# Two attentions with narrow heads: turning whole rows and stacking their parts through DRAM, against stacking in SBUF and turning the stacks

## The reference

```python
# layer 1 (the normed layer): LayerNorm over each head of 32 columns on q and k,
# the last 16 context rows form a second softmax whose result is added
q = _ln((x @ Wq + bq).reshape(b, s1, H, HD), qn_w, qn_b)          # H = 16, HD = 32
k = _ln(kv[..., :HD], kn_w, kn_b)
ctx = _attn(qT, k.transpose(0, 2, 1, 3), v.transpose(0, 2, 1, 3)) # softmax(q k' * HD**-0.5) v
...
# layer 2 (the rotary layer): q and k are rotated by tables of positions
q = apply_axial_rope((x @ Wq).reshape(b, n, 32, 16), pos_map)
k = apply_axial_rope(k.reshape(b, ctx_n, 32, 16), ctx_pos_map)
logits = jnp.einsum('bqhd,bkhd->bhqk', q, k) * scale
```

## Time and profile before

| what | us |
|---|---|
| three runs | 3720.03, 3726.92, 3727.14 (median 3726.92) |
| profiled execution: its span | 3721.0 |
| normed layer, one block in the steady part (1403.6 to 1549.6 is 6 blocks) | 24.33 |
| rotary layer, one block in the steady part (2243.1 to 2469.1 is 8 blocks) | 28.25 |
| normed layer, from its first load to its first scores | 53.0 (1245.7 to 1298.7) |
| rotary layer, from its first projection to its first scores | 26.3 (2110.9 to 2137.2) |

### The profile page before, as it was taken

One profiled execution on the slowest core, in us unless ns is written; L12 is line 12 of the kernel. 1 busy time (PEld: TensorE's weight loads), 2 busy tenths in 40 slices (PEclk: granted clock), 3 DMA queues, 4 the chain that ended last, 5 costly groups with the idle time before them and its releaser, 6 DMA issues.

```text
span 3721.0 us, 62085 instructions
## 1 busy us (share of the span) xinstructions
PE 3407.3 (92%) x23446; PEld 2808.9 (75%) x23446; DVE 2348.9 (63%) x4621; ACT 1666.9 (45%) x3641; POOL 1308.3 (35%) x1239
## 2 busy tenths in 40 slices
PE   7999999959999689988999899997889999999977
PEld 6899999937777456656998645554689999999865
DVE  6677777763323478866444466665667777777766
ACT  5666665531211155542222255554245555555531
POOL 1013334111243477732222356665422222222212
PEclk9999999978999899998999999999889999999989
DMA  3246665124645100001111000000000000000001
GB/s 130 80 135 222 225 227 181 42 80 168 241 176 188 69 27 28 11 5 69 35 35 38 1 4 3 4 3 19 28 6 18 13 18 18 18 7 19 12 1 48
DMA packets 94869, 246.53 MB, mean 66 GB/s; under 512 B 14448, under 2 KB 18672, under 8 KB 89840
## 3 DMA queue, kind: packets, MB, share of 16 engines
q1 hardware_dynamic: 88336, 222.12, 17.3%
q0 software_dynamic: 6240, 20.45, 1.6%
HBM read 364.95 MB, written 70.52 MB: 117 GB/s over the span
## 4 chain that ended last, share of the span: by engine, by line
PE 39%; DVE 6%; issue 3%; ACT 2%; POOL 2%; DMA 0%; SPq 0%; POOLq 0%; DVEq 0%; ACTq 0%
PE banks L104 34%; PE banks L214 4%; ACT P L78 1%; DVE xn L92 0%; POOL kst L87 0%; DVE X L87 0%; DVE st L270 0%; DVE PL L87 0%; DVE X L95 0%; POOL rs L87 0%; DVE KL L95 0%; DVE P L91 0%; ACT nkT L81 0%; POOL CL L87 0%; DVE XL L87 0%
## 5 line engine op out<-in xcount | busy, mean ns | idle before, releaser
L87 DVE TENSOR_TENSOR X<-X,banks 128x512 f32<-128x512 f32 x352 | 239.7, 682 | 192.9 <-PE banks L104 192.7
L98 DVE TENSOR_REDUCE nmx<-banks 128x4 f32<-128x1024 f32 (+2 forms) x256 | 239.1, 955 | 153.6 <-PE banks L104 151.6
L104 PE MATMUL banks<-XH,wqh 128*128 128x256 f32 x1024 | 291.9, 285 | 0.0
L104 PE MATMUL banks<-XL,wqh 128*128 128x256 f32 x1024 | 286.2, 279 | 0.0
L104 PE MATMUL banks<-XH,wql 128*128 128x256 f32 x1024 | 286.1, 279 | 0.0
L87 POOL TENSOR_TENSOR slo<-sraw,shi 128x512 fp32r<-128x512 f32 x96 | 126.9, 1322 | 379.3 <-ACT shi L81 351.2
L104 PE MATMUL banks<-XH,tT 128*128 128x256 f32 x1024 | 248.1, 286 | 8.8 <-DVE XL L87 5.9
L78 ACT ACTIVATE nPT<-banks 128x1024 f32<-128x1024 f32 x192 | 196.0, 1021 | 114.4 <-PE banks L104 113.9
L104 PE MATMUL banks<-XL,tT 128*128 128x256 f32 x1024 | 246.7, 284 | 0.0
L104 PE MATMUL banks<-woh,OH 128*128 128x512 f32 x512 | 219.2, 428 | 13.1 <-DVE OL L87 11.1
L78 ACT ACTIVATE P<-banks,nb,qst 128x256 f32<-128x256 f32 x256 | 141.0, 560 | 190.8 <-DVE nb L87 190.7
(11 more groups left out here) (435 smaller groups left out, 10480.5 us busy)
## 6 DMA issues: line engine op xcount, KB each, us to landing
WU<-expert_parts SPq DMA_DIRECT2D x39, 4096.0 KB
WD<-expert_parts SPq DMA_DIRECT2D x39, 2048.0 KB
sraw<-in_moe_w SPq DMA_DIRECT2D x96, 256.0 KB, 3.2
expert_parts<-shi SPq DMA_DIRECT2D x96, 256.0 KB
expert_parts<-slo SPq DMA_DIRECT2D x96, 256.0 KB
wqr<-in_L_xattn_Wq SPq DMA_DIRECT2D x16, 512.0 KB, 4.3
wor<-in_L_xattn_Wo SPq DMA_DIRECT2D x16, 512.0 KB, 5.5
sraw<-in_L_ffn_factors SPq DMA_DIRECT2D x32, 256.0 KB, 3.1
```

The costliest lines, as they stand in the source:

```text
L87: return self.e.tensor_tensor(out, a, b, op)
L98: return self.e.tensor_reduce(out, a, AX.X, op, **kw)
L104: return self.e.matmul(out, l, r, start=start, stop=stop, skip_group_check=skip)
```

## The change

Rows are turned plain, and split after. For each tile and kind (`kt`, `qt`) TensorE turns the 512 columns in one group of four, 32 groups or 128 turns a layer; ScalarE copies the group out of bank 7 twice, raw and rounded; POOL subtracts (`kl`, `ql`) to get the low part; SP writes high and low to a DRAM tensor `turned_parts` (`kw`, `qw`: two DMAs of 256 KB each, 512-byte rows). For each block SP then loads the stripes from DRAM into `nkT` and `nqT` (`rd`): 6 DMAs onto 32 partitions each (normed), 12 DMAs onto 16 partitions each (rotary), 1.57 MB a block either way, in rows of 1 KB. `rd` waits until both tiles' parts have landed and until the `st` steps of the block before the last are done; the first scores of the block wait for all of its loads. The selector stripes are made by POOL once and loaded into `nkT` at the start of the layer. The places of many steps change with it.

```diff
-            "k0": (-28, -20.5), "k1": (-28, -20), "q0": (-24.5, -18), "q1": (-22, -17), "q2": (-18.5, -13.5),
-            "k2": (-16, -14), "q3": (-18, -8), "k3": (-15, -5), "kp": -50, "krd": -49.5, "krp": -39.5, "qp": (-41, -39),
+            "kt": -47.5, "kl": -46.5, "kw": -45, "qt": -44.5, "ql": -43.5, "qw": -42, "rd": -17.5,
+            "kp": -56.5, "krd": -56, "krp": -53.5, "qp": (-53.5, -51.5), "qrd": -51.5, "qrp": -49, "vp": -17, "vb": -16,
...
+        self.TD = nc.dram_tensor("turned_parts", (2, NB, 2, 512, S), F32, kind="Internal").ap()
...
-    def wait_block(self, e, L, p, blk):
-        for q in "kq":
-            last = max(self.W[L]["turn"][f"{q}{2 + blk // 4}", (p // 2 * 2 + i, p % 2)] for i in range(2))
-            e.wait_ge(self.S["n_e" + q], last + 1)
+    def wait_block(self, e, L, p):
+        e.wait_ge(self.S[f"rd{p % 2}"], (96 if L == 1 else 192) * (p // 2 + 1))
+
+    def sp_parts(self, sp, L, kind, t):
+        S, b, i = self.S, t // 2, t % 2
+        dst = self.TD[0 if kind == "k" else 1][b].rearrange("a (c p) n -> p a c n", p=128)[:, :, :, 128 * i:128 * i + 128]
+        sp.wait_ge(S["n_lo" + kind], t + 1)
+        for a in range(2):
+            sp.dma(dst[:, a], self.parts_of(L, kind)[0][:, a].bitcast(F32)).then_inc(S[f"{kind}w{i}"], 16)
+
+    def sp_stacks(self, sp, L, p):
+        S, w, l1 = self.S, self.W[L], L == 1
+        b, hh = p // 2, p % 2
+        n = 32 if l1 else 16
+        for kind in "kq":
+            for i in range(2):
+                sp.wait_ge(S[f"{kind}w{i}"], 32 * (b + 1))
+        sp.wait_ge(S["n_st"], w["U"] * (p - 1))
+        for kind, tile, parts in (("k", "kT", (0, 1, 0)), ("q", "qT", (0, 0, 1))):
+            dst = w[tile][:, p % 2, :, :].bitcast(F32)
+            for s, a in enumerate(parts):
+                src = self.TD[0 if kind == "k" else 1][b, a, 256 * hh:256 * hh + 256, :].rearrange("(m e d) n -> e d m n", m=8, d=n)
+                for e in range(1 if l1 else 2):
+                    sp.dma(dst[64 * e + n * s:64 * e + n * s + n], src[e]).then_inc(S[f"rd{p % 2}"], 16)
...
-            if step in ("k1", "q1"):
...
-                pool.tt(part[2], src, part[0].bitcast(F32), ALU.subtract).then_inc(S["n_loq" if kind == "q" else "n_lok"], 1)
+            if step in ("kl", "ql"):
+                parts, raw = self.parts_of(L, step[0])
+                pool.wait_ge(S["n_e" + step[0]], t + 1)
+                pool.tt(parts[:, 1], raw[:], parts[:, 0].bitcast(F32), ALU.subtract).then_inc(S["n_lo" + step[0]], 1)
...
-            if step in ("k2", "k3", "q2", "q3"):
...
-                    x = (w["stq"] if q else w["stk"][:, t[0] % 2, :])[:, 512 * i + 128 * a:512 * i + 128 * a + 128].bitcast(F32)
-                    x = self.turn(pe, banks[7][:, 128 * a:128 * a + 128], x)
+            if step in ("kt", "qt"):
+                rows = self.rows_of(L, step[0], t)
+                self.wait_rows(pe, L, step[0], t)
+                self.wait_turned(pe, L, w["before7"][step, t])
+                for a in range(4):
+                    x = self.turn(pe, banks[7][:, 128 * a:128 * a + 128], rows[:, a, :])
...
+            if step in ("kt", "qt"):
+                kind = step[0]
+                parts, raw = self.parts_of(L, kind)
+                act.wait_ge(S["n_t" + kind], t + 1)
+                act.wait_ge(S["n_lo" + kind], t)
+                act.acopy(raw[:], z7)
+                if t:
+                    act.wait_ge(S[f"{kind}w{(t - 1) % 2}"], 32 * ((t + 1) // 2))
...
+                act.acopy(parts[:, 0], z7).then_inc(S["n_e" + kind], 1)
```

More of the change, by code:

```diff
@@ L161, in __init__ @@
         self.S = Sems(nc)
-        for name, first in (CHOICE_ON | CTX_ON).items():
+        for name, first in (CHOICE_ON | CTX_ON | TURNED_ON).items():
             self.S[name] = self.S[first]
@@ L1605, in narrow_list @@
                 put(base + at["mt"][i], "mt", (p, i))
-                for kind in ("k0", "k1", "k2", "k3", "q0", "q1", "q2", "q3"):
-                    put(base + at[kind][i] + first(kind, 2 * p + i), kind, (p // 2 * 2 + i, p % 2))
+            put(base + at["rd"], "rd", p)
         for t in range(NT):
@@ L1631, in narrow_before @@
         w["steps"] = self.narrow_list(L)
-        w["before6"], w["before7"], w["rope"], w["stack"], w["turn"] = {}, {}, {}, {}, {}
+        w["before6"], w["before7"], w["rope"] = {}, {}, {}
         last6 = last7 = None
@@ L1935, in wait_turned @@
             e.wait_ge(S["xh"], ln_at(2, a))
-        elif kind[0] == "q":
-            e.wait_ge(S["n_eq"], self.W[L]["turn"][use] + 1)
         else:
-            e.wait_ge(S["n_ek"], self.W[L]["turn"][use] + 1)
+            e.wait_ge(S["n_eq" if kind == "qt" else "n_ek"], a + 1)
     def wait_rows(self, e, L, kind, t):
@@ L1997, in sp_narrow @@
         back = self.OS[1:2 * T + 1, :].rearrange("(k t p) d -> t p k d", k=2, p=128)
+        m = 3 if l1 else 2
+        sp.wait_ge(S["n_sel"], m)
+        sel = w["sel"][:].rearrange("p j n -> p (j n)").unsqueeze(1)
+        keys = w["kT"][:].bitcast(F32).rearrange("p a (c j) n -> p (a c) (j n)", j=4)
+        for first, n in ((96, 8),) if l1 else ((48, 4), (112, 4)):
+            sp.dma(keys[first:first + n], sel.to_broadcast([n, 4, 1024])).then_inc(S["sel"], 16)
         for step, a in w["steps"]:
@@ L2013, in sp_narrow @@
                     sp.dma(dst[112:116], src[4:8].unsqueeze(1).to_broadcast([4, 4, 256])).then_inc(S[f"xs{k}"], 16)
+            if step in ("kw", "qw"):
+                self.sp_parts(sp, L, step[0], a)
+            if step == "rd":
+                self.sp_stacks(sp, L, a)
             if step == "mix":
@@ L2058, in pool_narrow @@
         k = 16 if l1 else 32
[L2059 to L2079 removed]
+        sel = w["sel"]
+        pool.e.memset(sel[:], 0.0).then_inc(S["n_sel"], 1)
+        pool.wait_ge(S["n_sel"], 1)
+        for first, c in ((0, slice(0, 240)), (4, slice(240, 256))) if l1 else ((0, slice(0, 256)),):
+            pool.e.affine_select(out=sel[:, :, c], in_=sel[:, :, c], compare_op=ALU.not_equal, fill=1.0, base=-first,
+                                 pattern=[[-1, 4], [0, c.stop - c.start]], channel_multiplier=1).then_inc(S["n_sel"], 1)
         if not l1:
@@ L2161, in pe_narrow, with heads @@
                              else wkv[:, c, 512 * e:512 * e + 512])
-        heads = lambda u: ((slice(0, 128), 2 * u), (slice(0, 128), 2 * u + 1)) if l1 else ((slice(0, 64), u), (slice(64, 128), u))
+        def heads(u, n):
+            return ((slice(0, n), 2 * u), (slice(0, n), 2 * u + 1)) if l1 else ((slice(0, n), u), (slice(64, 64 + n), u))
         for step, t in w["steps"]:
@@ L2290, in act_narrow @@
                 if t >= 8:
-                    act.wait_ge(S["n_loq"], max(w["stack"]["q", (t - 8, hh)] for hh in range(2)) + 1)
+                    act.wait_ge(S["n_tq"], t - 7)
                 act.wait_ge(S["ln_turned"], ln_at(2, t))
```

127 lines of the change are left out of this document (31 added, 96 removed), and 5 rows, old and new, of the table PLACES.

## The result

The changed kernel takes 3829.8 us (median of 4 runs, 3822.8 to 3832.7) against 3723.5 (3717.3 to 3727.1) for the kernel before: ratio 1.0284, 95% interval 1.0271 to 1.0297. It is 106 us slower. The forecast was 3708, 19 under the median of 3726.9 that it started from. The profiled execution has a span of 3830.8 us, 109.8 more than before's 3721.0.

A forecast was written before the change was run, and what follows sets the result against it. TensorE, busy nearly throughout both layers' steady blocks, was taken as the bound; -63 (rotary turns) + 43 (load wait) + 17 (rotary start) - 16 (normed layer) = -19 us, so 3702 profiled and 3708 measured, range 3660 to 3768.

The forecast's parts named there:

- Turns removed, rotary: Rotary layer, TensorE: 96 fewer turn groups and 16 waits for ScalarE's bank 7 copy gone, -63 us, 3.9 a block.
- Wait for the stack loads: Rotary blocks, before first scores: loads arrive after 13.6 us against 10.5 of cover, 3.1 us wait in 14 blocks, +43 us.
- Cover in the normed layer ... No wait, as long as SP is not late: Normed blocks: about 14 us of TensorE work covers stack loads taking 9.5 us in all, so no wait.
- 4 us lie between `mt` and its use: Maxima's DMAs queue behind the stack loads, but 4 us in the list before their use were to hide this.
- Normed body: Normed layer's blocks: 22.0 us each instead of 24.33, VectorE and POOL close behind TensorE; -33 us.
- keeps nothing: Rival: VectorE, POOL and SP's queue hold the normed block at 24.3 us; +14 in all, 3741 us, chance 0.17.
- Normed start: Normed layer up to first scores: first turn 12 us later, `qt0` ahead of `qp1` 7 more; sum +17, bounds 8 to 25.
- Rotary start: Rotary layer up to first scores: turn, copies, low part, write and 12 loads come first; +17 us, between 8 and 25.
- Serial loads: Rival: rotary loads run one after another, 6.7 us wait before each block's first scores; +36, 3763 us, chance 0.28.
- No wait at all: Rival: stack loads land as fast as issued, so rotary blocks never wait; -66, 3661 us, chance 0.15.

The follow-up runs named there:

- e6: e4 with each stack load cut into two halves, the first sent earlier, TensorE waiting only for the half it needs; ratio 0.9941 to the kernel before.
- e7: e4 with the same stack-load bytes sent onto three times as many partitions, so stacks hold other rows; ratio 0.9966 to the kernel before.
- e10: e8 with the normed layer's first turned scores of a half block moved behind the next half block's scores; 3692.0 us, ratio 0.9917 to the kernel before.
- e3: Changed kernel with SP issuing the loads of expert output earlier, later ones ahead of the stack loads; ratio 1.0140 to the kernel before.
- e2: Changed kernel with the maxima's DMAs issued by ScalarE behind its own copy instead of by SP; ratio 1.0253 to the kernel before.
- e8: Edits of e5 and e6 together, first normed loads at a place of their own; 3694.2 us, ratio 0.9902 to the kernel before.
- e5: e4 with first tiles' turn, low-part and store steps and first rotary stack loads moved in both layers' starts; ratio 1.0050 to the kernel before.
- e4: Changed kernel with the edits of e2 and e3 together; ratio 1.0109 to the kernel before.

## Why the prediction was wrong, step by step

- **Turns removed, rotary (-63).** Direction right, size wrong: without late loads the body is 39 us shorter (e6, e7, e10 agree within 0.5), 2.55 a block and not 3.9. TensorE's busy time fell by 2.55 us a block (219.66 / 8 to 199.23 / 8), not by the 3.20 that six groups take from start to start: start to start, the other instructions take 0.65 us a block more than beside the turns. And the 0.69 us wait for the copy out of bank 7 brought nothing: idle time is 0.79 us a block before and 0.80 after, now most of it for VectorE's nOT. I had subtracted a wait and not asked who is late next.
- **Wait for the stack loads (+43).** The mechanism, the place and the arrival were right: 13.6 us after the first issue, data of about 12.0 us (2420.2 to 2432.2), the last with some luck. The wait is 2.4 us a block (16.9 / 7) instead of 3.1, as the cover at this place was 12.1 us (2418.86 to 2430.92), not 10.5; 1.1 of it was a wait for VectorE's nOT, the attention's output. Over the body the loads cost 56 us (451.4 against 395.8), of which 40 are TensorE's waits for them: the first two are 5.9 and 3.9 us, the last but one 3.7. Together the two terms give +16.5 where -20 was forecast; more than half of the miss is the turns.
- **"Cover in the normed layer ... No wait, as long as SP is not late".** This is the step that failed, with 47 of the normed body's 66 us. The stack loads themselves were in time, as computed (1.3 us of wait in the whole layer, below); but SP was late, and I had given that condition no price. I had listed the maxima behind the stack loads and not SP behind POOL's low part, and not `ngt` behind the stack data. e3 removes the ring by SP's order alone: 47 us of body. The whole normed layer of the changed kernel, waits view:

```profile
POOL X L91 <- DMA ngt<-rows_out: 103.2, 15, 12.8
...
PE banks L108 <- DMA nqT<-nmT: 27.1, 15, 3.1
...
PEld banks L108 <- DMA nqT<-turned_parts: 1.3, 2, 0.8
```

- **"4 us lie between `mt` and its use".** This also failed, in the steady blocks, but no run shows that it cost time (e2, e10). Part of that time was turns, which the change takes away. At one place of the normed block it was 5.0 us before (1503.74 to 1508.77) and is 3.3 with the turns gone; e8's timeline:

```profile
1435.27 0.38 PE L219 MATMUL banks<-ident,nmx 128*8 128x128 f32 x2
1435.41 0.72 PE L108 MATMUL banks<-nkT,nqT 96*128 96x256 f32 x4
1435.97 0.64 PE L108 MATMUL banks<-nqT,nkT 104*128 104x256 f32 x4
1436.45 0.60 PE L219 MATMUL banks<-ident,ncb 128*128 128x128 f32 x4
1436.88 1.88 PE L108 MATMUL banks<-nwkv,CTX 128*128 128x512 f32 x4
1438.53 0.73 PE L108 MATMUL banks<-nqT,nkT 104*128 104x256 f32 x4
```

- **Normed body (-33).** Without the ring it is -14 (e3), -15 (e10). The block is 23.66 us (165.60 / 7), not 22.0; VectorE, named as the next bound, is busy 20.5 of it, and TensorE, busy 21.9, waits for its nV. TensorE's busy time fell by 1.7 us a block where I had taken off 2.9, and its idle time rose by 1.1 where I had taken off 0.7. That part of the rival "keeps nothing" was nearer than the forecast:

```profile
1429.00:1594.60 165.60, 153.40 (x1067) 87.08 (x1065) 143.28 (x250) 58.50 (x91) 128.64 (x87) 0.98 0.50 125
```

```profile
PE banks L108 <- DVE nV L91: 9.7, 7, 1.6
```

- **Normed start (+17, measured +32.4).** The two terms that I worked out are there in size: 12 us until the first turn (+13.1), 7 for `qt0` ahead of `qp1` (19.8 - 13.1 = 6.7). But the 12 are not SP's order alone: with that order mended (e3) the first turn gains 3 us, and the rest comes only when the low part of tile 1 moves as well (e5). Most of the missing 15 are the same ring once more: `kt2` waits 14.36 us for POOL's ncb, and POOL stands at a load `ngt` that was issued behind the first stack loads. In e3 the same wait is 5.1 us.
- **Rotary start (+17, measured +26.8).** From the first key projection to the scores it is 55.4 us, 10.9 of them at the end for the first loads. SP stood at `kw2` with them; e5 took 7.7 us off by the order. TensorE is busy 30.3 of the 55.4 at a clock of 0.78, and what the half clock adds there I had not counted.
- **The rivals.** None described what happened. Serial loads is refuted (it wanted a wait of 6.7 us and blocks of 31). "No wait at all" was right on what the loads allow once they are early, but gave the rotary body 63 us and not 39.
- **Open.** Where the last 12 us ahead of the rotary layer's first scores and 6 at the normed start of e10 sit, among the waits for the rotation, the parts' store and the clock, was not tried. Of the 56 us that the loads cost the rotary body, the 16 that are not waits for them are not placed. Whether 23.66 us is VectorE's limit or an order's is open too.

## What to carry to other kernels

When work moves from an engine to a DMA queue, walk the issuing engine's whole list: what stands behind each new wait, and whose data come behind the new bytes on the same queue; here that cost 47 us in a layer in which TensorE hardly ever waited for the new transfers themselves. Work taken out of a full engine was also cover, so subtract it from every latency that lay beneath it, and take no wait for gained without naming the next one: twice here (e2, e10) a wait that went came back under another name. Where a long load is late, issue its first half as soon as half of the buffer is free and let the reader wait for the half it needs: here that was worth 60 us. And before a few microseconds at a stage's start are put down to an edit, look at a mark ahead of that stage; here it moved by up to 5.

## What the runs showed of the hardware

- After the wait of 3.1 us shown above TensorE ran at its lower level, 1.2 GHz, for some 3.5 us; the windows before, right behind and after that place:

```profile
1517.00:1520.40 3.40, 3.40 (x19) 2.16 (x17) 3.20 (x4) 2.38 (x4) 3.40 (x3) 1.00 0.02 6
1523.60:1527.10 3.50, 3.48 (x10) 2.54 (x11) 1.37 (x3) 1.54 (x2) 1.81 (x2) 0.51 1.06 223
1527.10:1532.00 4.90, 4.90 (x47) 2.15 (x45) 3.96 (x9) 0.00 (x0) 0.00 (x0) 1.00 1.11 233
```

  A score group takes 1.22 us there instead of 0.64. So that wait of 3.1 us cost about 4.8 by my estimate (3.13 + 3.5 x 0.49). The group behind the rotary layer's wait of 1.51 us, shown above, ran at full speed (0.50 us).
- Twelve loads of 128 KB onto 16 partitions each, one behind the other, moved 1.57 MB in 12.0 us, 131 GB/s, where the earlier trace rows have 88 during a load that is over in 0.35 us: as far as so small a load can be compared, neighbours overlap in part. Onto 48 partitions (e7) a run of twelve is through 9.4 to 10.3 us after its first issue, for 12.6 to 14.3 (e4). The parts' store of 0.5 MB falls into the tail of both.
- A load of 64 KB lands in 2.3 us in the median, early or late in its run, where those of 128 KB go from 3.0 for the first to between 6 and 9 for the last: issued about every half microsecond, the large ones pile up and the small ones hardly do.
- SP issues a stack load in 0.43 to 0.47 us in the median. A single issue now and then takes much longer, up to 2.0 us (six in 4.03 us above). It does so in e6 too, where loads land in 2.3 us, so a long queue is not shown to be the reason.
